# Flamingo gated block, first cross attention: values over 512 query columns at once instead of twice 256

## The chip, the cores and the metric

The kernel runs on one core of one Trainium2 chip. A core has TensorE (PE, matmuls; PEld is its weight load), VectorE (DVE), ScalarE (ACT), GpSimd (POOL) and SyncE (SP, which here only issues DMAs). Each engine works through its own instructions in order, and semaphores tie the engines together. The metric is the device time of one execution in microseconds (us), the median of several runs.

## What is computed

Two gated cross-attention layers and two feed-forward layers on x of 2 batches x 512 tokens x 512. The change touches only the first cross attention. Cut to what matters, the reference is

```
q = (layernorm(x) @ Wq)   -> 16 heads of 128        k, v = ctx @ Wk, ctx @ Wv -> 8 heads of 128, each shared by 2 query heads
scores = einsum('bhtd,bhsd->bhts', q, k) / sqrt(128)        # 512 queries x 1024 keys
attn = softmax(where(mask, scores, -inf))
out = einsum('bhts,bhsd->bhtd', attn, v)                    # "values" below
x = x + tanh(g_xattn[0]) * (out @ Wo)
```

## The kernel before

The stage is cross_attention_0. One **turn** is one batch with one key/value head and its two query heads; there are 16 turns (h = 2g + b, batch b). A turn has NS = 8 **slots** n, one for each of its 2 heads x 4 tiles of 128 queries. Nothing plans the order: it is written out by hand, the same for every turn, and each engine runs its list. In slot n the engines do:

- PE: the scores of slot n (6 matmuls of 512 columns, L557: 2 halves of the keys x 3 products of a high and a low part of each operand, the tuple ACCURATE); then one piece of the projections for the *next* turn (slots 0 to 5: k0, q0, k1, q1, v0, v1; L488, L492, L498), which all go through one PSUM bank PJ; in slots 6 and 7 an output projection of the previous turn ahead of the transposes (L546, queries tile 1 and 2), also through PJ; then, in slots 6, 0, 2 and 4, a **values** group (L529); then 8 transposes of the probabilities of the slot four earlier (LAG = 4, L515); in slots 5 and 7 an output projection behind them (tile 0 and 3).
- DVE: a reciprocal of the row sum of the slot two earlier (L362); mask and row minimum of slot n, which empties the scores' PSUM pair (L385); the low part of the projection (L346 for k and q, L341 for v) or the addition of an output projection to x (L375), each of which frees PJ; in slots 0 and 4 the low part of a head's output (L395); then the low part of the transposed probabilities, two halves (L369), which frees the two PSUM banks of the transposes.
- ACT: the exponential of slot n (L429); the high part of a projection (L413); in slot 6 the high part of the next turn's v (L418), in slot 2 of the odd turns that of Wo (L442); in slots 0 and 4 the high part of a head's output (L438); then the high part of the transposed probabilities (L448, two halves), which DVE's L369 waits for.
- POOL: scales the probabilities (L464).

So a projection piece waits on PE until DVE has freed PJ (semaphores s_pjd and s_wd), and DVE's own instruction stands in DVE's list behind all that comes before it.

The values of one head are sums over 8 key tiles and 3 products, 24 matmuls for each stretch of query columns, into the PSUM bank OB. A query column can be used once its slot's transposes are emptied. Before, a head's 512 columns are made in two groups of 256 (`half`): the group m = 0 (head 0, first two query tiles) in slot 6 of the own turn, and m = 1, 2, 3 in slots 0, 2 and 4 of the next turn (VALUES = 6, `(n - VALUES) % 2 == 0`). The outputs are emptied in slots 0 and 4 (READY = [0, 4]).

The first turn has no work of a previous turn; the last has no projections for a next one; and behind the last turn comes a remainder with no scores, in which transposes, the last values groups and the four output projections follow each other.

Of the kernel before, what the change touches and what calls it, by code (L numbers as in the profile page):

```python
# [18 lines left out]
B, S, D = 2, 512, 512  # L19
# [3 lines left out]
QT = S // P  # L23
# [25 lines left out]
def program(nc, a, out):  # L49
    ctx = ExitStack()  # L50
    with ctx:
# [171 lines left out]
        def cross_attention_0():  # L223
# [3 lines left out]
            NKV, HPG, HD = 8, 2, 128  # L227
            TURNS = B * NKV
            NK = S2 // P
            GW = HPG * HD  # L230
            SCALE = 1.0 / float(np.sqrt(HD))
            NS = HPG * QT
            LAG = QT
            HALF = S // 2
            VALUES = LAG + 2

            READY = [VALUES + 2 * (2 * u + 1) - NS for u in range(HPG)]

            FRONT = ("k0", "q0", "k1", "q1", "v0", "v1")
            PROJECT = {n: name for n, name in enumerate(FRONT)}  # L240
# [14 lines left out]
            v = [[sb(f"x_v{i}{b}", [P, NK, HD], F32R) for b in range(B)] for i in range(2)]  # L255
            qT = [[[sb(f"x_qT{i}{b}{u}", [P, S], F32R) for u in range(HPG)] for b in range(B)] for i in range(2)]
            with ExitStack() as front:
# [4 lines left out]
            pT = [sb(f"x_pT{i}", [P, NK, S], F32R) for i in range(2)]  # L262
# [9 lines left out]
            PJ, OB, SC, TR = banks[0], banks[1], pairs[1:3], banks[6:8]  # L272
# [3 lines left out]
            s_pj, s_pjd, s_hi, s_of, s_oa, s_wd, s_sc, s_sm, s_ex, s_rt, s_pn, s_tr, s_ta, s_td = [  # L276
                sem(f"x_{n}") for n in ("pj", "pjd", "hi", "of", "oa", "wd", "sc", "sm", "ex", "rt", "pn", "tr", "ta", "td")]
# [6 lines left out]
            def until(engine, s, count):  # L284

                if not isinstance(count, int) or count > 0:
                    engine.wait_ge(s, count)
# [183 lines left out]
            def tensor(pe):  # L471
                pe.wait_ge(s_lnev, NT)
                pe.wait_ge(s_ctxev, PAIRS)
                pe.wait_ge(s_low, 2)
                pe.transpose(PJ[:, 0:B * NK], mrow[:, :], ident[0:B * NK, 0:B * NK]).then_inc(s_mtr, 1)
                pe.wait_ge(s_low, 3)

                def front(h, b, name):

                    i, j = FRONT.index(name), int(name[1])  # L480
                    if i:
                        pe.wait_ge(s_pjd, NF * h + i)
                    else:
                        until(pe, s_pjd, NF * h)
                        until(pe, s_wd, QT * (h - 1))
                    if name[0] == "k":
                        for c in range(VC):
                            mm = pe.matmul(PJ[:, :], wk[:, c, :], ctxT3[:, c, b * S2 + j * BANK:b * S2 + (j + 1) * BANK],  # L488
                                           start=(c == 0), stop=(c == VC - 1))
                    elif name[0] == "q":  # L490
                        for c in range(KC):
                            mm = pe.matmul(PJ[:, :], wq[:, c, j * HD:(j + 1) * HD], hT3[:, c, b * S:(b + 1) * S],  # L492
                                           start=(c == 0), stop=(c == KC - 1))
                    else:
                        for k in range(NK // 2):
                            tok = b * S2 + (j * NK // 2 + k) * P
                            for c in range(VC):
                                mm = pe.matmul(PJ[:, k * HD:(k + 1) * HD], ctxT3[:, c, tok:tok + P], wv[:, c, :],  # L498
                                               start=(c == 0), stop=(c == VC - 1))
                    mm.then_inc(s_pj, 1)  # L500

                pe.wait_ge(s_w, 16 * LOADS)
                for name in FRONT:
                    front(0, 0, name)

                def body(g, b, part):
                    h, before, own, ahead = B * g + b, part != "first", part != "after", part in ("first", "")

                    def transposes(n):
                        pe.wait_ge(s_pn, POOL * h + n + (2 if n >= 0 else 1))  # L510
                        for j in range(2):
                            until(pe, s_td, 2 * (NS * h + n) - 1 + j)
                            for k in range(NK // 2):
                                kk = j * NK // 2 + k
                                mm = pe.transpose(TR[j][:, k * P:(k + 1) * P], p[n % NS][:, kk * P:(kk + 1) * P], ident[:, :])  # L515
                            mm.then_inc(s_tr, 1)

                    def values(m, turn, b):

                        u, half = m // 2, m % 2  # L520
                        cols = slice(half * HALF, (half + 1) * HALF)
                        if half == 0:
                            until(pe, s_oa, 2 * (HPG * turn + u))
                        if m == 0:
                            pe.wait_ge(s_pn, POOL * turn + 1)
                        pe.wait_ge(s_td, 2 * (NS * turn + 2 * (m + 1)))
                        for n, (x0, x1) in enumerate(ACCURATE):
                            for k in range(NK):
                                mm = pe.matmul(OB[:, cols], v[x0][b][:, k, :], pT[x1][:, k, cols],  # L529
                                               start=(half == 0 and n == 0 and k == 0), stop=(half == 1 and n == 2 and k == NK - 1))  # L530
                        if half:
                            mm.then_inc(s_of, 1)

                    def project_out(t):

                        if t == 0:
                            pe.wait_ge(s_oa, 2 * HPG * h)
                            pe.wait_ge(s_wo, WO * (g + b))

                        if t == 0 and ahead:  # L540
                            pe.wait_ge(s_pjd, NF * (h + 2))
                        else:
                            pe.wait_ge(s_wd, QT * h + t)
                        for m, (x0, x1) in enumerate(ACCURATE):
                            for u in range(HPG):
                                mm = pe.matmul(PJ[:, :], oT[x0][u][:, t * P:(t + 1) * P], wo[x1][:, u, :],  # L546
                                               start=(m == 0 and u == 0), stop=(m == 2 and u == HPG - 1))
                        mm.then_inc(s_of, 1)

                    for n in range(NS):  # L550
                        if own:
                            if n == 0:
                                pe.wait_ge(s_pjd, NF * h + HI - 1)
                            until(pe, s_sm, NS * h + n - 1)
                            for j in range(2):
                                for m, (x0, x1) in enumerate(ACCURATE):
                                    mm = pe.matmul(SC[n % 2][:, j * BANK:(j + 1) * BANK], qT[x0][b][n // QT][:, n % QT * P:(n % QT + 1) * P],  # L557
                                                   kT[x1][b][:, j * BANK:(j + 1) * BANK], start=(m == 0), stop=(m == 2))
                            mm.then_inc(s_sc, 1)
                        if ahead and n in PROJECT:  # L560
                            if n == 0 and b == 1:
                                pe.wait_ge(s_w, 16 * LOADS * (g + 2))
                            front(h + 1, 1 - b, PROJECT[n])
                        if before and n in OUT_BEFORE:
                            project_out(OUT_BEFORE[n])
                        if n >= VALUES and own and (n - VALUES) % 2 == 0:
                            values((n - VALUES) // 2, h, b)
                        elif n < VALUES and before and (n - VALUES) % 2 == 0:
                            values(NS // 2 + (n - VALUES) // 2, h - 1, 1 - b)
                        if own if n >= LAG else before:  # L570
                            transposes(n - LAG)
                        if before and n in OUT_BEHIND:
                            project_out(OUT_BEHIND[n])

                turns(pe, body)
# [111 lines left out]
        def self_attention():  # L687
# [10 lines left out]
            SCALE = 1.0 / float(np.sqrt(HD))  # L698
            HALF = S // 2
            NS = HPG * QT  # L700
# [339 lines left out]
            def tensor(pe):  # L1040
# [40 lines left out]
                def body(g, b, part):  # L1081
# [10 lines left out]
                    def values(m, turn, b):  # L1092
# [7 lines left out]
                        for k in range(2 * half + 2):  # L1100
                            cols = slice(max(k * P, half * HALF), (half + 1) * HALF)
                            for n, (x0, x1) in enumerate(ACCURATE):
# [715 lines left out]
        def cross_attention_1():  # L1818
# [6 lines left out]
            SCALE = 1.0 / float(np.sqrt(HD))  # L1825
            HALF = S // 2
            LAG, RING = 3, 4
# [410 lines left out]
            def tensor(pe):  # L2238
# [6 lines left out]
                def body(j):  # L2245
# [56 lines left out]
                    def values(m):  # L2302

                        u, half = m // 2, m % 2
                        b, h = u // HPG, u % HPG
                        cols = slice(half * HALF, (half + 1) * HALF)
                        name = f"o{b}{h // 2}"
# [448 lines left out]
```

## Time and profile before

| | us |
|---|---|
| median of 3 runs | 3142.45 |
| the 3 runs | 3139.49, 3142.45, 3147.61 |
| span of the profiled execution (its own time, as the page gives it) | 3143.2 |
| the stage's score matmuls (L557), first and last start | 58.3 and 830.7 |
| one turn in the middle of the stage | 49.69 |

The span runs from the first instruction of the profiled execution to its last. The stage of the change is about a quarter of it. All times of the trace are us from the start of the span. In the trace a matmul group that follows another one without a pause is shown as starting a little before the other ends, so the length of a group is best read as its end (start + length) less the end of the group ahead of it; the chain view prints just that. The trace lists each fp32 matmul of the projections k and q as two, so 2 and 4 matmuls in the code are x4 and x8 there.

### The profile page before, as it was taken

What the parts mean: (1) busy time and instruction counts of PE and PEld (TensorE: products, weight loads), DVE (VectorE), ACT (ScalarE), POOL (GpSimd) and SP (SyncE); (2) the same over time, 40 slices, a digit from 0 to 9 for tenths busy, and PEclk for the clock granted to TensorE, in tenths of its full rate; (3) what the DMA queues carried; (4) which work ended last, traced back from release to release, by engine and by line L of the source; (5) the groups of instructions that cost most, each with busy time, mean ns of one, the idle gap of its engine ahead of it and who ended that gap; (6) DMA issues with size and microseconds to landing.
All of it is one profiled execution on the core that took longest, in us unless ns stands there. A gap on an engine that the chain in (4) does not pass through costs nothing.

```text
span 3143.2 us, 47718 instructions
## 1 busy us (share of the span) xinstructions
PE 2588.6 (82%) x15334; PEld 2096.9 (67%) x15334; DVE 1821.1 (58%) x3904; ACT 1530.5 (49%) x3062; POOL 1042.0 (33%) x1442
## 2 busy tenths in 40 slices
PE   6999999999859999999965888885378787878455
PEld 3787878778648777777745878774356575756332
DVE  2555555555455666655644443444477686857676
ACT  3544444444345555555633333331266574847644
POOL 0322232322224344444404555555233241414100
PEclk9999999999968999999977999998579798988778
DMA  2000000000010000000004444453300000020100
GB/s 75 18 17 10 17 7 17 17 10 7 1 37 18 17 17 17 17 17 0 17 33 151 147 154 163 150 167 111 92 15 1 22 1 22 1 70 7 71 7 20
DMA packets 91582, 137.98 MB, mean 44 GB/s; under 512 B 17152, under 2 KB 43776, under 8 KB 90816
## 3 DMA queue, kind: packets, MB, share of 16 engines
q1 hardware_dynamic: 84816, 114.66, 11.4%
q0 software_dynamic: 6640, 21.76, 2.0%
q8 instruction: 64, 1.05, 0.1%
q14 instruction: 62, 0.51, 0.1%
HBM read 119.62 MB, written 16.78 MB: 43 GB/s over the span
## 4 chain that ended last, share of the span: by engine, by line
PE 55%; issue 17%; DVE 12%; POOL 7%; ACT 7%; DMA 2%; DVEq 0%; ACTq 0%; SPq 0%; POOLq 0%
PE pair L529 6%; PE pair L1055 5%; POOL e_w L1429 4%; PE pair L2315 4%; PE pair L557 4%; PE pair L1105 4%; PE pair L492 4%; PE pair L1127 3%; PE pair L2299 3%; PE pair L515 3%; PE pair L2325 2%; PE pair L1089 2%; PE pair L498 2%; PE pair L488 2%; PE pair L1142 2%
## 5 line engine op out<-in xcount | busy, mean ns | idle before, releaser
L429 ACT ACTIVATE x_p<-x_p,x_least 128x1024 f32<-128x1024 f32 x128 | 147.2, 1150 | 307.8 <-DVE x_least L385 307.7
L1752 PE MATMUL pair<-m_h,e_w 128*128 128x320 f32 x1536 | 252.5, 328 | 47.8 <-DVE e_act L1690 45.3
L1752 PEld LDWEIGHTS pair<-m_h,e_w 128*128 128x128 f32 x1536 | 247.2, 204 | 53.5 <-DVE e_act L1690 49.2
L1429 POOL TENSOR_TENSOR e_w<-e_raw,e_w 128x2048 fp32r<-128x2048 f32 x48 | 220.5, 4596 | 187.0 <-ACT e_w L1395 187.0
L369 DVE TENSOR_TENSOR x_pT<-pair,x_pT 128x512 fp32r<-128x512 f32 x256 | 164.3, 684 | 122.6 <-ACT x_pT L448 122.6
L529 PE MATMUL pair<-x_pT,x_v 128*128 128x256 f32 x1536 | 210.8, 294 | 9.2 <-DVE x_pT L369 9.2
L529 PEld LDWEIGHTS pair<-x_pT,x_v 128*128 128x128 f32 x1536 | 195.1, 195 | 26.4 <-issue 18.3
L463 POOL TENSOR_TENSOR x_carry<-x_rtotal 128x1 f32<-128x1 f32 x128 | 24.7, 193 | 561.6 <-DVE x_rtotal L362 561.6
L967 ACT ACTIVATE s_p<-s_p,s_least 128x128 f32<-128x128 f32 (+3 forms) x256 | 143.3, 560 | 138.7 <-DVE s_least L878 138.6
L557 PE MATMUL pair<-x_kT,x_qT 128*128 128x512 f32 x768 | 207.3, 405 | 0.0
L2187 ACT ACTIVATE z_pT<-pair 128x512 fp32r<-128x512 f32 x256 | 143.0, 603 | 93.3 <-PE pair L2299 93.1
L2299 PE MATMUL pair<-ident,z_p 128*128 128x128 f32 x1024 | 151.4, 287 | 43.5 <-DVE z_pT L2091 43.5
L1105 PE MATMUL pair<-s_pT,s_v 128*128 128x256 f32 (+1 forms) x1152 | 160.6, 286 | 29.8 <-DVE s_pT L855 29.8
L2102 DVE TENSOR_REDUCE z_most<-pair 128x1 f32<-128x1008 f32 x128 | 153.9, 1202 | 53.0 <-PE pair L2335 53.0
L2091 DVE TENSOR_TENSOR z_pT<-pair,z_pT 128x512 fp32r<-128x512 f32 x256 | 163.5, 678 | 34.0 <-ACT z_pT L2187 33.3
L1105 PEld LDWEIGHTS pair<-s_pT,s_v 128*128 128x128 f32 x1152 | 153.4, 196 | 43.1 <-DVE s_pT L855 21.0
L1027 POOL TENSOR_TENSOR s_carry<-s_rtotal 128x1 f32<-128x1 f32 x256 | 49.8, 194 | 398.8 <-DVE s_rtotal L849 398.8
L2200 ACT ACTIVATE z_p<-pair,z_most 128x1008 f32<-128x1008 f32 (+1 forms) x256 | 174.4, 696 | 8.5 <-DVE z_most L2103 8.5
L2299 PEld LDWEIGHTS pair<-ident,z_p 128*128 128x128 f32 x1024 | 118.4, 145 | 86.7 <-DVE z_pT L2091 78.9
L2235 POOL TENSOR_SCALAR z_p<-z_p,z_rtotal 128x1008 f32<-128x1008 f32 (+1 forms) x256 | 174.8, 697 | 0.0
L855 DVE TENSOR_TENSOR s_pT<-pair,s_pT 128x128 fp32r<-128x128 f32 (+3 forms) x256 | 124.7, 488 | 79.8 <-ACT s_pT L953 79.8
L1055 PE MATMUL pair<-s_w,hT_attn 128*128 128x384 f32 x768 | 155.2, 352 | 6.7 <-POOL s_w L1006 6.7
(320 smaller groups left out, 6244.1 us busy)
## 6 DMA issues: line engine op xcount, KB each, us to landing
e_raw<-in_L_ffn_w SPq DMA_DIRECT2D x48, 1024.0 KB, 5.4
y_rows<-hslot SPq DMA_DIRECT2D x48, 256.0 KB, 6.6
f_raw<-in_L_ffn_w SPq DMA_DIRECT2D x2, 4096.0 KB, 15.0
s_wraw<-in_L_ffn_wq SPq DMA_DIRECT2D x9, 512.0 KB, 4.6
cslot<-in_ctx SPq DMA_DIRECT2D x16, 256.0 KB, 2.8
x_wq<-in_L_xattn_Wq SPq DMA_DIRECT2D x8, 512.0 KB, 3.5
x_woraw<-in_L_xattn_Wo SPq DMA_DIRECT2D x8, 512.0 KB, 3.6
s_woraw<-in_L_ffn_wo SPq DMA_DIRECT2D x8, 512.0 KB, 4.0
```

The costliest lines, as they stand in the source:

```text
L369: dve.tensor_tensor(pT[1][:, keys, q * P:(q + 1) * P], TR[j][:, :].rearrange("p (k n) -> p k n", n=P), pT[0][:, keys, q * P:(q + 1) * P].b ...
L529: mm = pe.matmul(OB[:, cols], v[x0][b][:, k, :], pT[x1][:, k, cols], start=(half == 0 and n == 0 and k == 0), stop=(half == 1 and n == 2 a ...
L557: mm = pe.matmul(SC[n % 2][:, j * BANK:(j + 1) * BANK], qT[x0][b][n // QT][:, n % QT * P:(n % QT + 1) * P], kT[x1][b][:, j * BANK:(j + 1) ...
L1055: mm = pe.matmul(o[:, 0:PW], hTa[x0][:, c, rows], w[x1][:, c, :], start=(n == 0 and c == 0), stop=(n == 2 and c == KC - 1))
L1105: mm = pe.matmul(OB[:, cols], v[b][:, k, first:first + 2, :].rearrange("p k d -> p (k d)"), pT[x1][:, k, cols], start=(i % 2 == 0 and half ...
L1429: pool.tensor_tensor(dst[1][:, :, :], raw[parity][:, :, :], dst[0][:, :, :].bitcast(F32), ALU.subtract).then_inc(s_lo, 1)
L1752: mm = pe.matmul(GU[m % 2][:, j * BANK:j * BANK + CAP], w[x0][:, c, m * P:(m + 1) * P], XS[s][x1][:, c, :], start=(n == 0 and c == 0), sto ...
L2091: dve.tensor_tensor(pT[1][:, k, cols], TR[i][:, :].rearrange("p (k n) -> p k n", n=P), pT[0][:, k, cols].bitcast(F32), ALU.subtract).then_ ...
L2102: dve.tensor_reduce(most[:, w, 0:1], SC[n % 2][:, 0:MAIN], AX.X, ALU.max, negate=True)
L2200: act.activation(p[w][:, cols], SC[n % 2][:, cols], ACT.Exp, bias=most[:, w, k:k + 1], accum_out=total[:, w, k:k + 1]).then_inc(s_ex, 1)
L2235: pool.tensor_scalar(p[w][:, cols], p[w][:, cols], rtotal[:, w, k:k + 1], 1.0, ALU.mult, ALU.mult).then_inc(s_pn, 1)
L2299: mm = pe.transpose(TR[i][:, k * P:(k + 1) * P], p[n % RING][:, kk * P:(kk + 1) * P], ident[:, :])
```

## The change

VALUES becomes the list of slots in which a whole head's values are made: (4u + 4 + 4) % 8 for u = 0, 1, which is slots 0 and 4 of the next turn. There 24 matmuls of 512 columns take the place of two groups of 24 of 256. Slots 2 and 6 have no values any more. READY, the slots in which the output is emptied, is [0, 4] as before, and the lists of DVE, ACT and POOL are the same as before.

```diff
-            HALF = S // 2
-            VALUES = LAG + 2
-
-            READY = [VALUES + 2 * (2 * u + 1) - NS for u in range(HPG)]
+            VALUES = [(QT * u + QT + LAG) % NS for u in range(HPG)]
+            READY = VALUES
+            assert all(QT * u + QT + LAG >= NS for u in range(HPG))
...
-                    def values(m, turn, b):
-
-                        u, half = m // 2, m % 2
-                        cols = slice(half * HALF, (half + 1) * HALF)
-                        if half == 0:
-                            until(pe, s_oa, 2 * (HPG * turn + u))
-                        if m == 0:
+                    def values(u, turn, b):
+
+                        until(pe, s_oa, 2 * (HPG * turn + u))
+                        if u == 0:
                             pe.wait_ge(s_pn, POOL * turn + 1)
-                        pe.wait_ge(s_td, 2 * (NS * turn + 2 * (m + 1)))
+                        pe.wait_ge(s_td, 2 * (NS * turn + QT * (u + 1)))
                         for n, (x0, x1) in enumerate(ACCURATE):
                             for k in range(NK):
-                                mm = pe.matmul(OB[:, cols], v[x0][b][:, k, :], pT[x1][:, k, cols],
-                                               start=(half == 0 and n == 0 and k == 0), stop=(half == 1 and n == 2 and k == NK - 1))
-                        if half:
-                            mm.then_inc(s_of, 1)
+                                mm = pe.matmul(OB[:, :], v[x0][b][:, k, :], pT[x1][:, k, :],
+                                               start=(n == 0 and k == 0), stop=(n == 2 and k == NK - 1))
+                        mm.then_inc(s_of, 1)
...
-                        if n >= VALUES and own and (n - VALUES) % 2 == 0:
-                            values((n - VALUES) // 2, h, b)
-                        elif n < VALUES and before and (n - VALUES) % 2 == 0:
-                            values(NS // 2 + (n - VALUES) // 2, h - 1, 1 - b)
+                        if before and n in VALUES:
+                            values(VALUES.index(n), h - 1, 1 - b)
```

In the new kernel the lines are one lower ahead of the values and five lower behind them: the values are L525 there, the transposes L514, the scores L552, the output projection L541, the projections k and q L487 and L491. Rows named ISA and REGISTER_ALU are waits and counters.

PE, slots 2 and 3 of a turn in the loop, from the projection k1 to the projection q1, before:

```order
L488 MATMUL pair<-ctxT,x_wk 128x512 x2
L287 ISA
L526 ISA
L529 MATMUL pair<-x_pT,x_v 128x256 x24
L510 REGISTER_ALU
L287 ISA
L515 MATMUL pair<-ident,x_p 128x128 x8
L287 REGISTER_ALU
L557 MATMUL pair<-x_kT,x_qT 128x512 x6
L482 REGISTER_ALU
L492 MATMUL pair<-hT_x,x_wq 128x512 x4
```

and now:

```order
L487 MATMUL pair<-ctxT,x_wk 128x512 x2
L509 REGISTER_ALU
L286 ISA
L514 MATMUL pair<-ident,x_p 128x128 x8
L286 REGISTER_ALU
L552 MATMUL pair<-x_kT,x_qT 128x512 x6
L481 REGISTER_ALU
L491 MATMUL pair<-hT_x,x_wq 128x512 x4
```

Between k1 and q1, which share the bank PJ, the values group is gone; transposes and scores are left.

PE, slots 6 and 7 of a turn in the loop, from the output projection of tile 1 to that of tile 2, before:

```order
L546 MATMUL pair<-x_wo,x_oT 128x512 x6
L287 ISA
L525 REGISTER_ALU
L526 REGISTER_ALU
L529 MATMUL pair<-x_pT,x_v 128x256 x24
L510 REGISTER_ALU
L287 REGISTER_ALU
L515 MATMUL pair<-ident,x_p 128x128 x8
L287 REGISTER_ALU
L557 MATMUL pair<-x_kT,x_qT 128x512 x6
L543 REGISTER_ALU
L546 MATMUL pair<-x_wo,x_oT 128x512 x6
```

and now:

```order
L541 MATMUL pair<-x_wo,x_oT 128x512 x6
L509 REGISTER_ALU
L286 ISA
L514 MATMUL pair<-ident,x_p 128x128 x8
L286 REGISTER_ALU
L552 MATMUL pair<-x_kT,x_qT 128x512 x6
L538 REGISTER_ALU
L541 MATMUL pair<-x_wo,x_oT 128x512 x6
```

The transposes of slot 6 stand directly behind the output projection of tile 1.

ACT, the same slot 6, exponential, high part of v and the two copies of transposed probabilities (the new kernel has the same rows in the same order, with line numbers one lower):

```order
L429 ACTIVATE x_p,x_total<-x_p,x_least 128x1024
L416 ISA
L418 ACTIVATE x_v<-cslot 128x1024
L447 ISA
L448 ACTIVATE x_pT<-pair 128x4x128
L447 REGISTER_ALU
L448 ACTIVATE x_pT<-pair 128x4x128
```

Nothing moved on ACT; it is PE that now comes to the transposes of this slot earlier.

## Rows read from the trace of the kernel before

**Rows 1.** Busy time by stretch: an even and an odd turn, two stretches near the end.

```profile
core 0: us, PE busy (x) PEld busy (x) DVE busy (x) ACT busy (x) POOL busy (x), PEclk, DMA share, GB/s
343.79:393.48 49.69, 49.64 (x289) 39.89 (x289) 28.23 (x52) 22.27 (x39) 12.63 (x17) 1.00 0.05 16
393.48:443.18 49.70, 49.64 (x289) 39.90 (x289) 28.22 (x52) 23.22 (x40) 14.95 (x18) 1.00 0.03 11
...
805.00:815.00 10.00, 7.79 (x43) 6.88 (x42) 4.98 (x10) 4.54 (x8) 4.91 (x5) 0.84 0.00 0
825.00:835.00 10.00, 10.00 (x63) 8.44 (x61) 5.22 (x11) 4.55 (x8) 2.02 (x3) 1.00 0.01 2
```

**Rows 2.** The chain that ended last, even turn: start, length, what.

```profile
345.73 2.87 PE pair L529 x24
348.61 0.87 PE pair L515 x8
349.48 1.39 PE pair L557 x6
...
363.43 3.43 PE pair L492 x8
...
386.36 0.61 ACT x_pT L448
```

**Rows 3.** Timeline of slot 2, even turn: start, length, engine, line, [idle before <- releaser].

```profile
354.94 1.64 PE L557 MATMUL pair<-x_kT,x_qT 128*128 128x512 f32 x6
...
356.86 1.22 DVE L385 CUSTOM_DVE_ANT_0 x_p<-pair,x_lower 128x1024 f32<-128x1024 f32 x1
...
358.12 1.15 ACT L429 ACTIVATE x_p<-x_p,x_least 128x1024 f32<-128x1024 f32 x1 [2.20 <-DVE x_least L385]
...
359.27 0.58 ACT L413 ACTIVATE x_kT<-pair 128x512 fp32r<-128x512 f32 x1
359.88 0.69 DVE L346 TENSOR_TENSOR x_kT<-pair,x_kT 128x512 fp32r<-128x512 f32 x1 [1.79 <-ACT x_kT L413]
```

**Rows 4.** Timeline, the first turn: the projection q1 behind k1 without values.

```profile
73.16 3.70 PE L492 MATMUL pair<-hT_x,x_wq 128*128 128x512 f32 x8 [0.47 <-DVE x_kT L346]
```

**Rows 5.** Timeline, all engines, slots 6 and 7 of the even turn.

```profile
380.11 1.53 PE L557 MATMUL pair<-x_kT,x_qT 128*128 128x512 f32 x6
...
381.48 1.55 PE L546 MATMUL pair<-x_wo,x_oT 128*128 128x512 f32 x6
...
384.33 1.04 ACT L418 ACTIVATE x_v<-cslot 128x1024 fp32r<-128x1024 f32 x1
...
386.99 1.29 DVE L369 TENSOR_TENSOR x_pT<-pair,x_pT 128x512 fp32r<-128x512 f32 x2 [3.17 <-ACT x_pT L448]
...
388.42 1.22 DVE L385 CUSTOM_DVE_ANT_0 x_p<-pair,x_lower 128x1024 f32<-128x1024 f32 x1
...
389.56 0.75 DVE L375 SCALAR_TENSOR_TENSOR x<-pair,tgate,x 128x512 f32<-128x512 f32 x1
...
390.37 1.66 PE L546 MATMUL pair<-x_wo,x_oT 128*128 128x512 f32 x6
```

**Rows 6.** Timeline, ACT, slot 2 of the odd turn.

```profile
409.43 1.05 ACT L442 ACTIVATE x_wo<-x_woraw 128x1024 fp32r<-128x1024 f32 x1
```

**Rows 7.** Timeline, last turn and the remainder behind it.

```profile
799.35 1.29 DVE L369 TENSOR_TENSOR x_pT<-pair,x_pT 128x512 fp32r<-128x512 f32 x2 [1.79 <-ACT x_pT L448]
...
812.14 4.63 PE L529 MATMUL pair<-x_pT,x_v 128*128 128x256 f32 x24 [2.21 <-DVE x_pT L369]
...
824.33 1.66 PE L546 MATMUL pair<-x_wo,x_oT 128*128 128x512 f32 x6 [1.51 <-DVE x L375]
...
840.84 1.16 PE L515 MATMUL pair<-ident,x_p 128*128 128x128 f32 x8 [1.23 <-DVE x_pT L369]
...
843.57 4.46 PE L529 MATMUL pair<-x_pT,x_v 128*128 128x256 f32 x24 [1.57 <-DVE x_pT L369]
...
852.61 3.13 PE L529 MATMUL pair<-x_pT,x_v 128*128 128x256 f32 x24 [1.48 <-DVE x_pT L369]
```

## The prediction, made before the changed kernel was run

> **What bounds the kernel now.** I read the busy time by stretch first, then the chain that ended last, then the timeline of single slots on all engines. A turn in the middle of the stage lasts 49.69 us, and in it TensorE is busy 49.64 at a granted clock of 1.00, its upper level of 2.4 GHz, while DVE has 28 and ACT 22 to 23 [rows 1]. The chain agrees: its pieces are PE groups end to end, values (L529) 2.87 us for 24 matmuls, transposes 0.87, scores 1.39, projection q 3.43 [rows 2]. So at first sight PE's streaming is the bound, and whatever shortens its list shortens the time. But the chain leaves PE once per turn: at 386.36 it runs through ACT's copy of transposed probabilities [rows 2] and on over DVE to the output projection of 390.37 [rows 5]. What the reader is to see in the timeline is how thin PE's cover is there. PE hardly waits because in each slot its work is a little longer than the loop that DVE and ACT must run, and the values are the part that made slots 2 and 6 long enough. A mean of 28 busy us in 50 says nothing about one slot.
>
> **The values themselves.** Before, a head costs 48 matmuls of 256 columns, 2 x 2.87 = 5.74 us, so 0.120 each [rows 2]. After, it costs 24 of 512 columns. The nearest row for that shape is the scores: 6 in 1.39, 0.232 each [rows 2], the same types, one weight load each. 24 x 0.232 = 5.56. So 256 more columns cost 0.112, and a matmul with its weight load has only 0.008 of fixed cost. A head saves 0.18 us, a turn 0.36, all 16 turns 5.8. Bounds for one matmul: 0.240, twice the 0.120, which saves nothing, and 0.214, half of one of q's 3.43 / 8 = 0.429, since q streams the same 512 columns in full fp32; a turn then saves 1.2.
>
> Here a rule speaks louder for the change than the trace does. A turn has 48 weight loads fewer; they are shown with 39.9 us of a turn's 49.7 busy [rows 1], yet they lie under the matmuls, as the 0.120 for 256 columns shows. The Trainium skill (TensorE: Matmul & The Clock Gate, The mechanism) says that a weight load overlaps with running matmuls only where the row group differs, and gives a load of 128 columns P / 1.2, about 107 ns (LDWEIGHTS). By that, as an estimate, 48 loads fewer would save 5.1 us per turn instead of 0.36. The trace disagrees: a load of 107 ns beside 256 columns doesn't fit into 0.120.
>
> **What is moved.** The four groups of 2.87 per turn become two of 5.56. Slots 0 and 4 grow by 2.69 each, 5.38 together. Nothing hides this: PE is on the path in both, and ACT and DVE only wait there. Slots 2 and 6 lose 2.87 each. The question of the whole case is how much of these 5.74 comes back.
>
> *Slot 2.* Times of the even turn. Scores end at 354.94 + 1.64 = 356.58. DVE's L385 ends at 358.08, ACT's exponential runs 358.12 to 359.27, only then ACT copies k1 (to 359.85), and DVE's L346 frees the bank PJ at 359.88 + 0.69 = 360.57 [rows 3]. All of this starts from the scores, not from k1. PE before the change needed PJ again at 363.43, when q1 begins [rows 2]: 2.86 us of slack, which is just the values group. Without it PE would be ready at 363.43 - 2.87 = 360.56 counted end to end, and it has to start q1 from rest: 0.06 after DVE (as 390.37 follows 389.56 + 0.75 [rows 5]), and 3.70 from there to its end, the length of a q1 that waited, against 3.43 of one that didn't [rows 2, 4]. q1 then ends at 360.63 + 3.70 = 364.33 instead of 366.86: 2.53 comes back, 0.34 is lost. That the wait occurs is seen in the first turn, where the same pieces stand without values and transposes: q1 waits there for the same L346, idle 0.47 [rows 4].
>
> *Slot 2 of the odd turns.* ACT copies Wo there as well, 1.05 us [rows 6], ahead of the transposed probabilities. Today the copy lies in the shade of the values. Now it delays the copy of the probabilities to its own end, and with it DVE's L369, the row minimum of slot 3 behind that, the exponential of slot 3, and so the emptying of q1, which v0 waits for. I put the exponential's end 0.95 after q1's end; two copies, 0.58 and 0.69, bring the release of PJ about 0.1 past the point at which v0 is due, and v0 starts from rest, another 0.2: 0.3 more in odd turns. Bounds 0 and 0.6.
>
> *Slots 6 and 7.* The output projection of tile 1 ends at 381.48 + 1.55 = 383.03. Before, values followed, and the transposes ended at 386.76, ACT's copies began at 386.36 behind their first half [rows 2]. Now the transposes would end at 383.90, but ACT is busy until 384.33 + 1.04 = 385.37 with the high part of v, which stands in its list ahead of the copies [rows 5]. So the copies start at 385.38, 0.98 earlier and not 2.87. Everything behind is a queue on DVE without a gap: L369 from 386.99 (its two halves to 388.28), the row minimum of slot 7 from 388.42, and the addition of output projection 2 from 389.56 to 390.31, after which PE starts output projection 3 at 390.37 [rows 5]. PE has its other work done earlier (scores, output projection 2, transposes of slot 7) and waits, about 0.5 ahead of the second half of these transposes and about 1.3 ahead of the output projection. 0.98 comes back, 1.89 is lost. The row minimum of slot 7, the exponential behind it and the next turn's k0 keep their distances, so nothing more is lost or made up.
>
> *A turn in sum.* Even: 5.38 - 2.53 - 0.98 = +1.87 us. Odd: +2.17. The turns 1 to 14 have all four slots with projections, 7 of each kind: 7 x 1.87 + 7 x 2.17 = +28.3.
>
> *Both ends.* In the first turn slot 6 gives back 0.3 instead of 1. The last turn has no projections; a slot there is bound by a loop of DVE and ACT: row minimum 1.22, exponential 1.15, one copy 0.61, L369 1.29 [rows 2, 3, 7], with the gaps between them 4.3 us. Where values stand in such a slot they add to it. Slots 0 and 4 cost 2.69 each there, slot 2 gives back about 1.8 (the copy of Wo takes its place in part), slot 6 about 2.4. In the remainder the first whole group adds 2.69; the middle one of 4.46 disappears, and the transposes follow each other at 0.61 + 1.29 + 0.2 = 2.1, which brings the last values from 852.61 to some 4.9 earlier [rows 7]; the last group adds 2.69. Sum: 10.8 - 1.8 - 2.4 - 4.9 = +1.7, less 0.3: +1.4. The clock can add to this: behind idle times of 2.21 and 1.57 the groups took 4.63 and 4.46 instead of 3.13 [rows 7], so a long group may meet that 1.5 once or twice.
>
> **Sum.** +28.3 + 1.4 = +29.7 us. Against its own execution, a span of 3143.2, this is 3172.9; the median of the three runs is 0.75 lower, so 3142.45 + 29.7 = 3172.1. I say 3172. A measurement of this kernel can tell about 0.3%, 9.4 us, from no change.
>
> **The rivals.**
>
> *PE's streaming is all that counts.* If the waits of slots 2 and 6 were hidden, the 0.36 a turn would stand alone: -5.8 us, 3136.6, within 0.3%. For it speaks that PE is busy 99.9% of a turn [rows 1]; against it rows 4 and 5, where the queues of ACT and DVE are seen end to end. It would take ACT's copy ahead of its high part of v, which its list forbids. Chance 0.05. Half way between, where one of the two waits is much shorter than I work out: 3146 to 3157, chance 0.08, part of it within 0.3%.
>
> *The weight loads bound PE.* From rows, with the weight load's mean of 39.9 / 289 = 0.138 us [rows 1] as a fixed cost of each matmul, 48 fewer save 6.6 a turn instead of 0.36: 3172 - 15 x 6.3 = 3078. But a whole matmul with its load takes 0.120 [rows 2], so the chance is 0.02. By the 107 ns of the Trainium skill's page (TensorE: Matmul & The Clock Gate, LDWEIGHTS) it would be 3172 - 15 x 4.7 = 3101, as an estimate.
>
> *The clock falls in every turn.* Behind output projection 2 PE will be idle 1.8 us with only transposes between. In the trace an idle time of 1.51 left the granted clock at 1.00 (825 to 835), 2.21 brought it to 0.84 (805 to 815) [rows 1, 7], and two waits of 1.23 and 1.57 with transposes between them, the pattern that now arises in slot 7, were followed by the slow group of 4.46. If 1.2 GHz is granted behind each of them, a turn loses 1.3 to 1.5 more: 14 x 1.4 = +20, 3192. Decided by which of these stretches the new one turns out to be like. Now and then, at some of the turns: +2 to +8, which is inside my case. Every turn: chance 0.08.
>
> **Chances and range.** My case, 3160 to 3184, 0.77; the half-way case 0.08; the clock 0.08; streaming alone 0.05; weight loads 0.02. The range 3156 to 3188 holds my case and the edges of its neighbours, a little over 0.8. Faster by over 0.3%: 0.02. Within 0.3% (streaming alone, and the low part of the half-way case): 0.08. Slower by over 0.3%: 0.90.
>
> **What would show it.** In the changed profile: a turn of 51.5 to 51.9 us; values groups of 5.5 to 5.6; q1 idle 0.1 to 0.4 for L346's result in every turn; DVE's addition of an output projection as the cause of a PE wait of 1.2 to 1.4, and DVE's L369 as that of one of 0.3 to 0.6, once a turn each; ACT going from the high part of v straight to the copies; a granted clock that stays at 1.00 in the middle. I am wrong if a turn is shorter than 49.7, if these waits name other engines, or if the values take less than 5.3.

## The result, and the profile after

The changed kernel is slower by 0.64%: ratio 1.0064, 95% interval 1.0047 to 1.0082, from medians of 3167.25 (7 runs) and 3147.61 us (7 runs of the kernel before, the 3 shown ahead among them). That is 20 us, with an interval of 15 to 26. The prediction said 3172, +29.7, so the sign and the mechanism held and the size was half as large again as it should have been. The time itself, 3167.25, lies inside the range of 3156 to 3188 and only 5 us below 3172; half of the error is hidden there by luck, since the seven runs put the kernel before at 3147.61, 5 us above the 3142.45 that the prediction added to. Two runs are left out of the ratios here, one of move_only with 8251 us and one of the kernel before with 5103 us, both slow executions.

The profiled execution has a span of 3160.7 us (3162.49 with what lies around it) against 3143.2. PE's busy time is the same (2588.9 against 2588.6 us), with 768 matmuls fewer; the weight loads are shown busy 46 us less (2051.3 against 2096.9), DVE 8 and ACT 4 less. Nobody works more: what was added is waiting. The busy time of each engine (share of the span, instructions) on its page:

```profile
PE 2588.9 (82%) x14566; PEld 2051.3 (65%) x14566; DVE 1813.0 (57%) x3904; ACT 1526.2 (48%) x3062; POOL 1041.7 (33%) x1442
```

The chain that ended last, from the k0 in slot 0 of an even turn over the next k0 to the one behind it (start, length, what):

```profile
351.51 1.98 PE pair L487 x4
...
361.20 3.45 PE pair L491 x8
...
370.20 0.70 DVE x_kT L345
370.94 3.70 PE pair L491 x8
...
378.69 5.50 PE pair L525 x24
...
394.82 0.95 ACT x_v L417
395.77 0.49 ACT x_pT L447
397.64 1.12 DVE x_p L384
...
401.77 0.75 DVE x L374
402.57 1.98 PE pair L487 x4
404.55 5.47 PE pair L525 x24
...
453.66 1.98 PE pair L487 x4
```

351.51 to 402.57 is the even turn, 51.06 us, and 402.57 to 453.66 the odd one, 51.09; the mean of the 12 turns from 147.16 to 760.04 is 51.07, against 49.69 before [rows 1]. The values take 5.46 to 5.50 for a whole head, against 2 x 2.87 [rows 2]. The chain now leaves PE in two places: at q1 (370.94), which follows DVE's low part of k1, and in slots 6 and 7, where it runs over ACT's high part of v, the copy of transposed probabilities and DVE's row minimum, and from there over slot 7's exponential and copies to DVE's addition of output projection 3 (401.77), which frees PJ for k0. Output projection 3 itself waits for the same row minimum (next rows). Before, the chain over the even turn had no high part of v in it.

The timeline of slots 6 and 7 of the even turn (start, length, engine, line, what, [idle before <- releaser]) answers to [rows 5]:

```profile
393.24 1.03 PE L514 MATMUL pair<-ident,x_p 128*128 128x128 f32 x8
...
394.73 1.04 ACT L417 ACTIVATE x_v<-cslot 128x1024 fp32r<-128x1024 f32 x1
...
395.68 1.06 ACT L447 ACTIVATE x_pT<-pair 128x512 fp32r<-128x512 f32 x2
396.28 1.29 DVE L368 TENSOR_TENSOR x_pT<-pair,x_pT 128x512 fp32r<-128x512 f32 x2 [2.08 <-ACT x_pT L447]
397.03 1.25 PE L514 MATMUL pair<-ident,x_p 128*128 128x128 f32 x8
...
397.56 1.21 DVE L384 CUSTOM_DVE_ANT_0 x_p<-pair,x_lower 128x1024 f32<-128x1024 f32 x1
...
398.69 0.75 DVE L374 SCALAR_TENSOR_TENSOR x<-pair,tgate,x 128x512 f32<-128x512 f32 x1
...
399.49 1.65 PE L541 MATMUL pair<-x_wo,x_oT 128*128 128x512 f32 x6 [1.21 <-DVE x L374]
```

What to see: PE has turned slot 6's probabilities by 394.27 (393.24 + 1.03), but ACT begins to copy them at 395.68, when it is through with v. From there DVE goes without a gap, and PE stands 1.21 us until DVE has emptied PJ. The waits view of PE, from 136 to 800 us, gives the same for 13 turns and names no other wait:

```profile
PE pair L541 <- DVE x L374: 15.7, 13, 1.2
```

Where the time is, from the traces: the stage's last output projection ends at 864.64 + 1.67 = 866.3 before and at 889.0 after, 22.7 later; the rest of the kernel, which is the same code, takes 2276.9 in the one profile and 2271.7 in the other. That part differs by up to 14 us from execution to execution (2271.7 to 2285.5 in the profiles of this study, though its code is the same in all), so the length of a turn is the sharp measure here, and the whole time the blunt one. 14 turns x 1.38 = 19.3 of the 22.7; the other 3.4 lie at the two ends, 0.5 of them because the stage began later in this execution (first scores at 58.82 instead of 58.32).

### The profile page after: what moved, and what is told of

It reads as the page before. It is cut to its first block, busy times and chain, and to the rows that moved or that the text cites. A ratio compares the mean times of both kernels' runs of the same rounds, so it can differ in the third digit from the quotient of the medians.

```text
span 3160.7 us, 46154 instructions
## 1 busy us (share of the span) xinstructions
PE 2588.9 (82%) x14566; PEld 2051.3 (65%) x14566; DVE 1813.0 (57%) x3904; ACT 1526.2 (48%) x3062; POOL 1041.7 (33%) x1442
## 4 chain that ended last, share of the span: by engine, by line
PE 51%; issue 18%; DVE 13%; ACT 8%; POOL 7%; DMA 2%; DVEq 1%; ACTq 0%; SPq 0%; POOLq 0%
PE pair L525 6%; PE pair L1048 5%; POOL e_w L1422 4%; PE pair L2308 4%; PE pair L1098 4%; PE pair L491 4%; PE pair L1120 3%; PE pair L552 3%; PE pair L2292 3%; PE pair L2318 2%; PE pair L1082 2%; PE pair L497 2%; PE pair L1135 2%; PE pair L514 2%; POOL e_rows L1603 1%
## 5 line engine op out<-in xcount | busy, mean ns | idle before, releaser
L552 PE MATMUL pair<-x_kT,x_qT 128*128 128x512 f32 x768 | 208.2, 407 | 0.0
L525 PE MATMUL pair<-x_pT,x_v 128*128 128x512 f32 x768 | 190.4, 405 | 4.8 <-DVE x_pT L368 4.8
L525 PEld LDWEIGHTS pair<-x_pT,x_v 128*128 128x128 f32 x768 | 145.3, 191 | 41.6 <-issue 12.5
```

The lines of the kernel that those rows point to most:

```text
L525: mm = pe.matmul(OB[:, :], v[x0][b][:, k, :], pT[x1][:, k, :], start=(n == 0 and k == 0), stop=(n == 2 and k == NK - 1))
```

## Experiments

The theory: the width is a small gain, and the place is the loss. Cover is the work that PE has while another engine runs the list at whose end something is freed for PE. Slots 2 and 6 were covered by their values, and of 2 x 2.87 us only part comes back, because ACT and DVE have their own lists to run there. The rivals: the wide matmuls themselves bring the loss; each head's move costs the same; PE's idle time in slot 7 is DVE's own work and not ACT's order.

A turn's length below is the distance of two k0 groups in the chain or timeline of the kernel's profile.

**Only the move.** Both halves with 256 columns, one after the other, in slots 0 and 4.

```diff
-                        for n, (x0, x1) in enumerate(ACCURATE):
-                            for k in range(NK):
-                                mm = pe.matmul(OB[:, :], v[x0][b][:, k, :], pT[x1][:, k, :], ...)
+                        for half in range(2):
+                            cols = slice(half * S // 2, (half + 1) * S // 2)
+                            for n, (x0, x1) in enumerate(ACCURATE):
+                                for k in range(NK):
+                                    mm = pe.matmul(OB[:, cols], v[x0][b][:, k, :], pT[x1][:, k, cols], ...)
```

> The new places with the old width: both halves of 256 columns of a head directly one after the other in slots 0 and 4, 48 matmuls of 256 instead of 24 of 512. The theory (the loss is the place, the width is a gain): a turn of 51.08 us with 2 x 5.47 for values becomes one with 2 x 5.74, so 51.6 us, and the whole about 28 us over the kernel before; the waits in slots 2 and 7 stay at 0.34 and 1.2. Rival (the wide matmuls themselves bring the loss, for instance by keeping PSUM or the weight path busy): a turn goes back to 49.7 to 50.0.

Measured: 1.0100 of before (1.0068 to 1.0132, from three runs), some +31 us. A turn is 51.64 us, from two rows of its chain, and 48 matmuls take 5.75 to 5.76:

```profile
352.91 1.98 PE pair L487 x4
354.89 5.75 PE pair L527 x48
...
404.55 1.98 PE pair L487 x4
```

So the move alone costs 51.64 - 49.69 = 1.95 us a turn, and the width gives back 51.64 - 51.07 = 0.57, some 0.28 for each of the two heads. The rival falls: the 512 columns are the good half of this change.

**One head at a time.** Head 0 whole in slot 0, nothing in slot 6, head 1 in halves; and the mirror, head 1 whole in slot 4, nothing in slot 2, head 0 in halves. `whole` is the changed kernel's values, `values` that of before.

```diff
+                        if before and n == 0:
+                            whole(0, h - 1, 1 - b)
+                        elif before and n in (2, 4):
+                            values(1 + n // 2, h - 1, 1 - b)
```
```diff
+                        if n == 6 and own:
+                            values(0, h, b)
+                        elif n == 0 and before:
+                            values(1, h - 1, 1 - b)
+                        elif n == 4 and before:
+                            whole(1, h - 1, 1 - b)
```

> Head 0 as in the changed kernel (24 matmuls of 512 columns in slot 0, none in slot 6), head 1 as before (halves in slots 2 and 4). The theory: slot 6 gives back only 1.26 of its 2.87 us, slot 0 grows by 2.60, so a turn of 49.69 + 1.34 = 51.0 us and the whole 20 us over before; PE waits for the addition of output projection 2 about 1.2 us per turn, and q1 doesn't wait. Rival (each head's move costs the same half of 1.39): 50.4 us and 10 us.

> Head 1 as in the changed kernel (24 matmuls of 512 columns in slot 4, none in slot 2), head 0 as before (halves in slots 6 and 0). The theory: slot 2 gives back 2.53 of its 2.87 us, slot 4 grows by 2.60: a turn of 49.76 us and the whole within 2 us of before; q1 waits 0.34 per turn, slots 6 and 7 are as before. Rival (each head's move costs the same): 50.4 us and 10 us.

Measured: head 0 1.0057 (1.0036 to 1.0079), a turn of 51.01; head 1 1.0008 (0.9993 to 1.0024), turns of 49.72 and 49.78 by turns, in the mean 49.75. The k0 rows of the two chains, head 0 first:

```profile
349.37 1.99 PE pair L488 x4
...
400.38 1.99 PE pair L488 x4
```
```profile
344.65 1.98 PE pair L488 x4
...
360.77 0.70 DVE x_kT L346
361.52 3.70 PE pair L492 x8
...
394.37 1.98 PE pair L488 x4
```

+1.32 and +0.06 add up to the +1.38 of both. The first has the same wait as the changed kernel (PE for the addition, 1.2 us in 13 turns, 15.7 in sum), the second the wait of q1 and its 3.70, and no other that the kernel before lacks. Of its 2.87 us, slot 2 gives back 2.60 - 0.06 = 2.54 and slot 6 2.60 - 1.32 = 1.28, and the rival of equal halves falls; the prediction had 2.53 and 0.98.

**ACT's order in slot 6**, on the changed kernel and, as a control, on the kernel before: the high part of v behind the copies of transposed probabilities.

```diff
-                        if ahead and n == SPLIT:
-                            high_values(h + 1, 1 - b)
...
                                 act.activation(pT[0][:, j * NK // 2:(j + 1) * NK // 2, q * P:(q + 1) * P], ...)
+                        if ahead and n == SPLIT:
+                            high_values(h + 1, 1 - b)
```

> The changed kernel, with ACT's high part of v put behind the two copies of transposed probabilities in slot 6 instead of ahead of them; nothing else. The theory: the copies start when the exponential ends, 1.0 us earlier, and with them all of DVE's queue up to the addition of output projection 2; a turn of 50.1 us, and the whole 14 us less than the changed kernel, some 6 over before. Rival (DVE's own work in slots 6 and 7 is too long for what PE has there): no change, 51.1 us, since the order on ACT doesn't matter.

> The kernel before with the same edit on ACT as v_behind (the high part of v behind the two copies in slot 6). A control. The theory: no change, 49.69 us a turn, since there the copies wait for PE's transposes, 1.0 us after ACT has finished with v. Rival (the edit is good in itself, cover or not): about 1 us a turn less, 14 us in all.

Measured: on the changed kernel 1.0015 of before (1.0005 to 1.0025), 15 us less than the change alone, a turn of 50.1; on the kernel before 1.0003 (0.9991 to 1.0015), a turn of 49.70. Both as the theory has it, and the rival (DVE's own work) falls. In the changed kernel with this edit the copy starts right behind the exponential, and PE's wait for the addition is halved, 8.8 us in 14 turns (timeline, slots 6 and 7):

```profile
386.80 1.15 ACT L428 ACTIVATE x_p<-x_p,x_least 128x1024 f32<-128x1024 f32 x1 [3.37 <-DVE x_least L384]
...
387.94 1.06 ACT L445 ACTIVATE x_pT<-pair 128x512 fp32r<-128x512 f32 x2
...
388.90 1.06 ACT L417 ACTIVATE x_v<-cslot 128x1024 fp32r<-128x1024 f32 x1
...
391.76 1.66 PE L541 MATMUL pair<-x_wo,x_oT 128*128 128x512 f32 x6 [0.61 <-DVE x L374]
```

It is the cover that made the order on ACT unimportant before; take the cover away and 1.04 us of ACT's list is worth 0.97 us a turn.

**ACT's order in slot 2**, on the changed kernel: k1's copy ahead of the exponential.

```diff
+                        if ahead and n == 2:
+                            front(h + 1, 1 - b, PROJECT[n])
                         if own:
                             act.wait_ge(s_sm, NS * h + n + 1)
...
-                        if ahead and n < HI - 1:
+                        if ahead and n < HI - 1 and n != 2:
```

> The changed kernel, with ACT's copy of k1 ahead of the exponential of slot 2 instead of behind it. The theory: DVE's low part of k1, and so q1, no longer waits for row minimum and exponential: the 0.34 us go in even turns (50.7 instead of 51.08); in odd turns ACT's copy of Wo now delays the exponential of slot 3 enough to hold up v0 by about as much, so 50.7 to 51.1 there. The whole 2 to 5 us less than the changed kernel. Rival (the start of q1 is held by something else, such as its weights or the PSUM bank's turn-round): no turn changes.

Measured: 1.0052 (1.0032 to 1.0073), 4 us below the changed kernel's 1.0064, but the intervals overlap. Even turns are 50.72, as expected, odd turns 51.28, outside the expected 50.7 to 51.1 and longer than without the edit; with a mean of 51.00 the gain is 0.07 a turn, and the stage ends at 889.1 as before the edit:

```profile
352.30 1.98 PE pair L489 x4
...
371.69 3.43 PE pair L493 x8
...
403.02 1.98 PE pair L489 x4
...
428.39 2.05 PE pair L499 x16
...
454.30 1.98 PE pair L489 x4
```

In the even turn q1 is back at 3.43, no wait. In the odd turn v0 waits 0.29 for DVE's low part of q1 and starts from rest (2.05 instead of 1.78): the time was given back at the next projection, whose release stands behind the exponential of slot 3, and that comes late. To tell whether ACT's copy of Wo does that, it was put in slot 0, where ACT waits for the values anyway:

```diff
-                        if own and b == 1 and n == SPLIT_WO:
+                        if own and b == 1 and n == 0:
```

> k1_first with the copy of Wo in slot 0 in the same way. The theory: both kinds of turn 50.73 us. Rival as in best: odd turns stay at 51.27.

Measured in a single run of 3159.13 us, of which only the trace is used: all turns 50.73 or 50.74; the k0 rows of an odd one:

```profile
397.83 1.98 PE pair L489 x4
...
448.56 1.98 PE pair L489 x4
```

The rival, POOL's low part of Wo, moved forward with the copy, by some 6 us (419.94 instead of 426.05), so this run alone doesn't exclude it. But the chain of k1_first's odd turn runs from ACT's copy of Wo over the transposed probabilities, the row minimum and the exponential of slot 3 to v0, and POOL isn't in it.

**A wait that was there before.** In the kernel before, k0 waits in every turn for the addition of output projection 3, which stands on DVE behind the low part of the transposed probabilities: it takes 1.98 us, against 1.72 where it doesn't wait (chain of the kernel before):

```profile
392.65 0.75 DVE x L375
...
393.44 1.98 PE pair L488 x4
```

Added first:

```diff
+                        if before and n == NS - 1:
+                            add_out(OUT_BEHIND[n])
                         if own if n >= LAG else before:
                             evacuate(n - LAG)
-                        if before and n in OUT_BEHIND:
+                        if before and n in OUT_BEHIND and n != NS - 1:
```

> The kernel before with DVE adding output projection 3 ahead of the low part of the transposed probabilities in slot 7, instead of behind it. The theory (a PJ release that stands behind other DVE work is what PE waits for): the wait of 0.33 us of k0 in every turn goes, 49.36 us a turn, 5 us in all. Rival: the values group of slot 0 then waits for the transposed probabilities and the turn stays at 49.7.

Measured: a turn of 49.38 in the trace, as expected (k0 1.72 at 342.65, and again at 392.03); the whole 1.0003 (0.9990 to 1.0016), so 14 x 0.31 = 4.3 us can't be told in the whole time.

**The parts that pay, together.** head1_whole, k1's copy first, the addition first; and then the copy of Wo in slot 0 too.

> The parts that should pay, together: head 1 whole with 512 columns in slot 4 and head 0 in halves in slots 6 and 0 (as head1_whole), ACT's copy of k1 ahead of the exponential in slot 2, DVE's addition of output projection 3 first in slot 7. The theory: 49.75 - 0.34 (even turns; 0 to 0.34 in odd ones) - 0.33 = 49.1 to 49.4 us a turn, 5 to 9 us less than before (0.998). Rival (one of the waits comes back behind the next instruction of the same engine): 49.7.

> head1_k1_add with ACT's copy of Wo in slot 0 of the odd turns, ahead of the head's output, where ACT waits for the values anyway, instead of in slot 2. The theory: the odd turns lose their wait for v0 and come down from 49.67 to the 49.10 of the even ones; the stage 4 us less than head1_k1_add and 8 less than before, 0.9974 of it. Rival (the odd turns are longer for another reason, such as POOL's low part of Wo): they stay at 49.67.

Measured: without the copy of Wo 0.9994 (0.9982 to 1.0005), turns of 49.10 and 49.67; the odd ones missed the expected 49.1 to 49.4 and are where the rival had them, one wait come back. With the copy of Wo moved **0.9981 (0.9968 to 0.9994)**, expected 0.9974: 6 us less than the kernel before and 26 less than the changed one, all turns 49.15:

```profile
340.06 1.72 PE pair L492 x4
...
364.07 5.50 PE pair L546 x24
...
389.21 1.72 PE pair L492 x4
```

Its chain over this turn holds nothing but PE. Its stage ends 7.7 us earlier than before (858.6 against 866.3). Of the 0.54 us a turn, 0.24 are head 1 (5.50 instead of 2 x 2.87) and 0.3 are k0, which no longer waits.

## Why the prediction was right in kind and too high in size

**The values.** Predicted 0.232 us for a matmul of 512 columns, measured 5.47 / 24 = 0.228. The scores still take 1.38 to 1.40 for six in the changed kernel, so a group of six was no measure of a long one; why it costs 0.004 more a matmul isn't shown. A turn's growth in slots 0 and 4 is 5.20 instead of 5.38. So the fixed cost of a matmul with its weight load is 2 x 0.1196 - 0.228 = 0.011, and the sum of the width alone is 0.54 (0.57 in the experiment) instead of 0.36. The kernel with the move only measures the loads: 24 matmuls and loads fewer a head, 48 a turn, are worth 0.57 us a turn. By the rule of the Trainium skill (TensorE: Matmul & The Clock Gate, The mechanism) that loads overlap only in other row groups, and with its 107 ns for a load, it would have been, as an estimate, 5.1. The trace disagrees with the two together; which of them fails here no run shows, and the same section also lets a load go ahead into a background weight buffer.

**Slot 2.** Predicted: q1 from rest, 3.70, and 0.34 lost. Measured: q1 ends 3.77 behind the scores ahead of it instead of 3.43, 0.34. Most of this is the 3.70 of a group that starts from rest; the wait itself is 0.07. The chain scores, row minimum, exponential, copy, low part was read to 0.01 us, and in the even turns of k1_first the 0.34 is gone.

**Slot 2 in odd turns.** Predicted 0.3 more, measured 0.02 at v0 (1.80 instead of 1.78). The rows show why (timeline of ACT in the changed kernel's odd turn):

```profile
425.23 1.15 ACT L428 ACTIVATE x_p<-x_p,x_least 128x1024 f32<-128x1024 f32 x1 [2.07 <-DVE x_least L384]
...
426.38 0.58 ACT L412 ACTIVATE x_qT<-pair 128x512 fp32r<-128x512 f32 x1
```

q1 ends at 425.72, ACT's copy of it starts 0.66 later and not 0.95. I had worked this out as a sum of shown starts and lengths, each with 0.1 too much, since on ACT a following activation starts before the shown end of the one ahead (420.67, 421.14, 422.09 for lengths of 0.58, 1.05), and had given q1 no part of its own delay as cover. 0.66 is just within what v0 tolerates. k1_first, which takes the delay of q1 away, brings the 0.5 out, and k1_wo removes it: the mechanism was right, its start was missed by 0.3 us.

**Slots 6 and 7.** This is the term that was mis-sized most. Predicted: 0.98 comes back and 1.89 is lost. Measured: 0.40 for the transposes and 1.21 for output projection 3, 1.61 lost, 1.26 comes back. Of the 0.28 between them, 0.08 is again ACT: its copy starts at 395.68, not at the shown end of v, 395.77. And 0.15 is a wait I took for DVE's own time: I kept the distance of 1.43 between DVE's low part (386.99) and the row minimum (388.42) of [rows 5], but that distance had a wait for PE's scores in it: slot 7's ended at 388.14 and DVE went on at 388.34, the same 0.20 behind them as in slot 6 (381.64, 381.84), where the trace names the scores as the cause. After, they end at 395.65 and hold nobody up; the distance is 1.28 (396.28 to 397.56). A distance between two instructions of one engine holds only as long as the second isn't waiting for someone whose time the edit changes.

**The ends.** Predicted +1.4, with 1.5 more for each long group that meets the low clock. Measured 3.4, or 2.9 from the first scores on. The first turn, predicted 0.3 shorter, is 1.05 longer; the next grew by 0.6 only; and from the last shown k0 on (741.30 before, 760.04 after; turn 14, the last turn and the remainder) it is 3.9 against a predicted 1.87 + 1.7. The long groups did meet the low clock twice, and the slow scores of the first turn are a third place:

```profile
92.27 1.62 PE L514 MATMUL pair<-ident,x_p 128*128 128x128 f32 x8 [2.66 <-DVE x_pT L368]
...
93.54 2.82 PE L552 MATMUL pair<-x_kT,x_qT 128*128 128x512 f32 x6
```
```profile
832.92 7.30 PE L525 MATMUL pair<-x_pT,x_v 128*128 128x512 f32 x24 [2.34 <-DVE x_pT L368]
...
856.43 5.73 PE L525 MATMUL pair<-x_pT,x_v 128*128 128x512 f32 x24 [0.86 <-DVE x_pT L368]
...
871.25 7.17 PE L525 MATMUL pair<-x_pT,x_v 128*128 128x512 f32 x24 [1.57 <-DVE x_pT L368]
```

PE idled 2.66 us in the first turn, behind the slot 6 that lost its values; before, its values stood there and the clock was 1.00 in the same stretch. The granted clock by stretch (length, PE busy, clock, DMA) in the changed kernel:

```profile
85.00:97.00 12.00, 9.34 (x43) 0.86 0.21 66
...
394.00:402.00 8.00, 6.77 (x34) 1.00 0.00 0
...
833.00:840.00 7.00, 7.00 (x24) 0.76 0.00 0
...
871.00:880.00 9.00, 7.34 (x25) 0.81 0.00 0
```

0.86, 0.76 and 0.81 are means over parts at 2.4 and parts at 1.2 GHz. Against the 5.73 of a group that started from rest and wasn't slowed (856.43), the two long groups lost 1.6 and 1.4 us, the scores 1.2 against 1.62. The kernel before lost about as much at such places: its groups of 4.27 (at 800.78), 4.63 and 4.46 are 1.1, 1.5 and 1.3 above 3.13. Nor is it fixed where that happens. The control before_v_behind has the same PE list, and the first two of these groups took 3.11 and 3.14 there, behind idle times of 2.35 and 2.19 that are 2.35 and 2.21 in the kernel before; its end, from the k0 of 740.50 on, is 2.9 us shorter. And in head0_whole 2.67 us of idle time in the first turn were followed by scores of the usual length:

```profile
91.26 1.16 PE L515 MATMUL pair<-ident,x_p 128*128 128x128 f32 x8 [2.67 <-DVE x_pT L369]
...
92.17 1.62 PE L569 MATMUL pair<-x_kT,x_qT 128*128 128x512 f32 x6
```

So the 3.4 of the ends is known to some 3 us only, and what the clock has in it stays open.

**The sum.** Per turn 5.20 - 2.53 - 1.26 = 1.41, measured 1.38. I said 1.87 and 2.17, mean 2.02; over 14 turns 28.3 against 19.3. Of the 9.0 too many, 2.5 are the width (14 x 0.18), 3.9 slots 6 and 7 (14 x 0.28), 2.0 the odd turns (7 x 0.28); 0.6 is left over. All three errors lie on the same side. In two of them I took shown lengths or distances on ACT and DVE as hard where they had 0.1 to 0.15 us of give; the width was a group of six taken for a long one. The turn of 51.07 lies below the 51.5 to 51.9 that I had named as a sign, and the values' 5.46 to 5.50 at the lower edge of the 5.5 to 5.6. The other signs came as named: q1 behind DVE's low part of k1, the two waits in slots 6 and 7 with their causes, ACT's order and the clock.

**The rivals.** Streaming alone, -5.8 us: its width term is there, and larger (0.54 a turn instead of 0.36), its assumption fails: with both heads moved no kernel here has a chain of PE alone; best has one, with one head moved and three edits on ACT and DVE. The weight loads as a fixed cost of 0.138 each: 6.6 us a turn were predicted from it, 0.57 measured. The clock in every turn: not seen, the granted clock is 1.00 in 394 to 402, around waits of 0.40 and 1.21, and in each of the 12 turns from 147 to 760.

## What to carry to other kernels

Joining two groups of a bound engine can save their fixed cost and still lose, because the places they are taken from lose their cover; before moving work, ask of each slot how long the other engines' lists take from its first event to the release that the bound engine needs: only what the bound engine's work exceeds this by comes back. Here one of two moves was nearly free (0.06 us a turn) and the other cost 1.3, so try them one at a time. And look for a short task that stands in an engine's list ahead of one that others wait for: here it cost nothing under cover (49.70 against 49.69) and 0.97 of its 1.04 us without.

## What was new about the hardware

- Copies on ACT that follow each other are shown overlapping by about 0.1 us (v at 394.73 for 1.04, the next copy at 395.68), so such a queue is shorter than the sum of its rows.
- A matmul with its own weight load costs 0.1196 us at 256 columns and 0.228 at 512, at the upper clock, types as in the values here: if the columns cost the same in both, 0.011 us is fixed.
- Idle times of PE of 2.66, 2.34 and 1.57 us were followed by groups partly at 1.2 GHz, and in other executions 2.67, 2.35 and 2.19 us were not (head0_whole, before_v_behind); one of 1.21 us with transposes ahead of it left 2.4 GHz in each of the 12 turns read.
